# Opening of a wavelet-attention and FFN kernel: chunks 2 and 3 analysed by even and odd tokens

## The reference

```python
for _ in range(NUM_LEVELS):              # 2
    l = dwconv(low, h_filter)[:, ::2]
    h = dwconv(low, g_filter)[:, ::2]
    highs.append(h)
    low = l
low = linear_attention(low, NUM_HEADS)   # keys = elu + 1, kv = sum of keys * values over all tokens
for h, L in zip(reversed(highs), reversed(lens)):
    low = dwconv(up_l, h_synth) + dwconv(up_h, g_synth)
x = layernorm(x + layer_norm(x + low) ...)
x = layernorm(x + (silu(x @ wg.T) * (x @ wu.T)) @ wd.T)
```

## Time and profile before

| | |
|---|---|
| median of 3 runs | 1214.51 us (1214.37 to 1216.5) |
| the profiled execution, its own time | 1215.94 us |
| its span | 1214.1 us |
| PE, DVE, ACT, POOL busy | 98%, 81%, 55%, 25% |

### The profile page before, as it was taken

One profiled execution on the slowest core, in us unless ns is written; L12 is line 12 of the kernel. 1 busy time (PEld: TensorE's weight loads), 2 busy tenths in 40 slices (PEclk: granted clock), 3 DMA queues, 4 the chain that ended last, 5 costly groups with the idle time before them and its releaser, 6 DMA issues.

```text
span 1214.1 us, 19304 instructions
## 1 busy us (share of the span) xinstructions
PE 1188.0 (98%) x6352; PEld 622.1 (51%) x6352; DVE 984.6 (81%) x1981; ACT 672.3 (55%) x1395; POOL 303.7 (25%) x730
## 2 busy tenths in 40 slices
PE   7989999999999999999999999999999999999997
PEld 6868644455445544455444444454445444454443
DVE  7997999998999989996997779867997689845331
ACT  5853754578446853577346644566346644565342
POOL 0013223052223413052122413142213313131101
PEclk9999999999999999999999999999999999999999
DMA  6777421213202220212102210211111310110000
GB/s 233 240 185 161 161 64 56 96 62 132 71 27 96 96 71 18 96 61 97 35 27 96 75 57 19 101 66 53 35 47 75 105 33 12 41 56 1 8 29 35
DMA packets 51869, 91.86 MB, mean 76 GB/s; under 512 B 8896, under 2 KB 28608, under 8 KB 50880
## 3 DMA queue, kind: packets, MB, share of 16 engines
q1 hardware_dynamic: 50048, 86.01, 21.3%
q0 software_dynamic: 1728, 4.72, 2.2%
HBM read 65.99 MB, written 25.19 MB: 75 GB/s over the span
## 4 chain that ended last, share of the span: by engine, by line
PE 82%; DVE 7%; ACT 4%; issue 3%; POOL 2%; DMA 1%; SPq 0%; POOLq 0%; DVEq 0%; ACTq 0%
PE ps_up L641 12%; PE ps_up L642 12%; PE ps_gate L641 12%; PE ps_gate L642 12%; PE ps_down L659 12%; PE ps_down L660 12%; PE ps_x L584 2%; PE ps_y L602 2%; DVE l L1229 1%; DVE h L1229 1%; DMA q_scratch<-keys 1%; PE ps_x L563 1%; POOL rs L1158 1%; PE ps_down L806 1%; DVE hid L1229 1%
## 5 line engine op out<-in xcount | busy, mean ns | idle before, releaser
L659 PE MATMUL ps_down<-w,hid 128*128 128x512 f16 x768 | 291.2, 379 | 1.2 <-DVE hid L1618 1.0
L660 PE MATMUL ps_down<-w,hid 128*128 128x512 f16 x768 | 291.1, 379 | 0.0
L641 PE MATMUL ps_up<-x_hi,w 128*128 128x512 f16 x760 | 288.2, 379 | 1.0 <-DVE h_f L1631 1.0
L641 PE MATMUL ps_gate<-x_hi,w 128*128 128x512 f16 x760 | 288.2, 379 | 0.5 <-ACT h_f L1102 0.5
L642 PE MATMUL ps_gate<-x_lo,w 128*128 128x512 f16 x760 | 288.1, 379 | 0.0
L642 PE MATMUL ps_up<-x_lo,w 128*128 128x512 f16 x760 | 288.1, 379 | 0.0
L1102 ACT ACTIVATE h_f<-ps_gate 128x512 f32<-128x512 f32 x192 | 113.9, 593 | 205.2 <-PE ps_gate L642 204.2
L1631 DVE SCALAR_TENSOR_TENSOR h_f<-ps_up,h_f 128x512 f32<-128x512 f32 x192 | 130.9, 685 | 110.4 <-PE ps_up L642 97.6
L1094 ACT ACTIVATE hid<-h_f 128x512 f16<-128x512 f32 x192 | 119.8, 624 | 42.5 <-DVE h_f L1631 42.4
L1618 DVE TENSOR_TENSOR hid<-h_f,hid 128x512 f16<-128x512 f32 x192 | 130.9, 682 | 1.9 <-ACT hid L1094 1.0
L641 PEld LDWEIGHTS ps_up<-x_hi,w 128*128 128x128 f16 x760 | 74.4, 98 | 91.4 <-DVE h_f L1631 1.9
(11 more groups left out here) (247 smaller groups left out, 1728.5 us busy)
## 6 DMA issues: line engine op xcount, KB each, us to landing
xt<-x_tok SPq DMA_DIRECT2D x64, 256.0 KB, 2.6
out<-x SPq DMA_DIRECT2D x64, 256.0 KB, 2.0
xa<-x_chan SPq DMA_DIRECT2D x28, 515.0 KB, 5.2
xb<-x_chan SPq DMA_DIRECT2D x7, 2060.0 KB, 7.6
w<-weights POOLq DMA_DIRECT2D x12, 384.0 KB, 9.7
att<-den SPq DMA_DIRECT2D x32, 129.5 KB, 2.7
q_in<-q_scratch SPq DMA_DIRECT2D x7, 518.0 KB, 4.8
h_in<-h_scratch SPq DMA_DIRECT2D x7, 518.0 KB, 5.8
```

The costliest lines, as they stand in the source:

```text
L641: pe.matmul(ps_gu[k % 2][g][:, :], w, x1_hi[:, b, c, :], start=(c == 0), stop=False)
L659: pe.matmul(ps_d[t % 2][:, :], h_hi[:, k, t * P:(t + 1) * P], w, start=(k == 0), stop=False)
L660: mm = pe.matmul(ps_d[t % 2][:, :], h_lo[:, k, t * P:(t + 1) * P], w, start=False, stop=(k == NH - 1))
```

## The change

- **x in another layout.** For chunks 2 and 3 of rounds 0 to 4 the host also gives `x_phase`. A chunk is split in two halves h of 64 channels; the even tokens of such a half lie in partitions 0 to 63, the odd ones in 64 to 127. `load_pro` takes its place in SP's list, with the same bytes. Round 0's copy lies in `x1`, so `xb` of chunks 2 and 3, which the closing reads, is loaded with two more DMAs of 515 KB behind rounds 1 and 2.
- **Two taps in one matrix.** `phase_diag(c, h, n)` is 128x64: 64 channels out, and both parities in, so it carries two taps. `conv1` and `conv2` write even outputs (or half 0) to partitions 0 to 63 of a bank and odd ones (or half 1) to 64 to 127, which are two column groups of the array, in turn. A chunk takes 8 matmuls of 257 or 256 columns as before, each on half of the array's columns. Rounds 0, 3 and 4 add one matmul of one column for each half, which writes the edge's zero. The constants come with a DMA (`phase_sb`) between `coef` and `ident`.
- **Chunk 2 of level 2** goes from DVE and ACT to PE: `conv2(a, 2)` behind `pro_kv(a-1)`, into ps_down1, with `pro_out2_copy(a, 2)`. `pro_band_taps(a, 2)` and `pro_band_firsts(a, 2)` are gone. kv moves from ps_down1 to ps_x.
- **Order of ACT.** `pro_l1(a+1, 0)` and `(a+1, 1)` stand at the end of round a, ahead of `pro_keys(a, 0)`. `pro_diags` makes 28 matrices instead of 24, ten in each of rounds 1 and 2, eight in round 3.

The core of the diff:

```diff
+        def phase_diag(c, h, n):
+            at = (c - 2) * 8 * P + (h * 4 + n) * HALF
+            return diag_z[:, at:at + HALF]
...
+        def l1_phase_of(a, c):
+            return l1_of(a)[:, c, :].rearrange("p (h n) -> p h n", h=2)
...
             sp.dma_start(coef[:, :, 0:16], taps).then_inc(ld_taps, 16)
+            sp.dma_start(phase_sb[:, :], phase).then_inc(ld_taps, 16)
             sp.dma_start(ident[:, :], identity).then_inc(ld_taps, 16)
...
+                if a in (1, 2):
+                    sp.dma_start(xb[:, a + 1, :], x_chan[:, 0, a + 1, :]).then_inc(ld_xb0, 16)
...
-                pro_conv(ps_gu[c - 2], xb if a == 0 else xa, c, 0, span_l1(a)).then_inc(pro_conv1, 1)
+                x = x_phase_of(a, c)
+                for h in range(2):
+                    bank = ps_gu[c - 2][h]
+                    spans = [[0, LP], [0, LP]]
...
+                    for k in range(2):
+                        for out_phase, (lo, hi) in enumerate(spans):
+                            r = out_phase + k
+                            mm = pe.matmul(bank[out_phase * HALF:(out_phase + 1) * HALF, lo:hi], phase_diag(c, h, k),
+                                           x[:, h, 2 * lo + r:2 * (hi - 1) + r + 1:2], start=(k == 0), stop=(k == 1))
+                mm.then_inc(pro_conv1, 1)
+            def conv2(a, c):
...
                 for g in range(2):
-                    for k in range(4):
-                        mm = pe.matmul(ps_d[0][:, g * M2:(g + 1) * M2], diag(3, 4 * g + k),
-                                       l1_of(a)[:, 3, k:k + 2 * M2 - 1:2], start=(k == 0), stop=(k == 3))
+                    for k in range(2):
+                        for h in range(2):
+                            mm = pe.matmul(ps_d[3 - c][h * HALF:(h + 1) * HALF, g * M2:(g + 1) * M2],
+                                           phase_diag(c, h, 2 * g + k), x[:, h, k:k + M2], start=(k == 0),
+                                           stop=(k == 1))
...
             for a in range(NPRO):
-                pro_l1(a, 0)
-                pro_l1(a, 1)
-                if a > 0:
+                if a == 0:
+                    pro_l1(a, 0)
+                    pro_l1(a, 1)
+                else:
                     pro_keys(a - 1, 1)
...
-                pro_band_firsts(a, 2)
...
-                    pro_diags(8 * (a - 1), 8)
-                pro_out2_copy(a)
+                    pro_diags(10 * (a - 1), 10)
+                pro_out2_copy(a, 3)
+                pro_out2_copy(a, 2)
+                if a < PER_BATCH:
+                    pro_l1(a + 1, 0)
+                    pro_l1(a + 1, 1)
                 pro_keys(a, 0)
...
-                pro_band_taps(a, 2)
                 if 0 < a < PER_BATCH:
                     pro_kv_add(a - 1)
```

More of the change, by code:

```diff
@@ L42 @@
 HEAD = 32
+HALF = P // 2
+XP = XW // 2
+LP = LW // 2
 LN_EPS = 1e-5
@@ L166, with mixer_ffn @@
 COPIES = HEAD // CHUNK_HEADS
-def mixer_ffn(nc, x_tok, x_chan, taps, gamma, beta, edge, weights, identity, block_mask, head_mask, out):
+def mixer_ffn(nc, x_tok, x_chan, x_phase, phase, taps, gamma, beta, edge, weights, identity, block_mask, head_mask, out):
     q_dram = nc.dram_tensor("q_scratch", [P, BATCHES, NC, SEQ // 4 + 3], F32, kind="Internal").ap()
@@ L460, in _ @@
             sp.dma_start(coef[:, :, 0:16], taps).then_inc(ld_taps, 16)
+            sp.dma_start(phase_sb[:, :], phase).then_inc(ld_taps, 16)
             sp.dma_start(ident[:, :], identity).then_inc(ld_taps, 16)
+            load_pro(0, 3)
+            for c in range(2):
+                sp.dma_start(xb[:, c, :], x_chan[:, 0, c, :]).then_inc(ld_x0[c], 16)
+            load_pro(0, 2)
             for c in (3, 0, 1, 2):
-                sp.dma_start(xb[:, c, :], x_chan[:, 0, c, :]).then_inc(ld_x0[c], 16)
-            for c in (3, 0, 1, 2):
-                load_xa(1, c)
+                load_pro(1, c)
             for dst, src in ((mask[:, :], block_mask), (head_of[:, :], head_mask),
@@ L719, in pro_turn @@
                     pe.wait_ge(turn_out, NC * (a - 1) + c + 1)
+                if c == 0 and a > 0:
+                    pe.wait_ge(kv_added, a)
                 if c == 2:
@@ L764, in h_conv @@
                     pe.wait_ge(turn_out, NC * PER_BATCH)
[L765 removed]
+                    pe.wait_ge(diag_syn_ready, 8)
+                    pe.wait_ge(ld_xb0, 32)
                 else:
@@ L808, in pro_s @@
                 mm.then_inc(pro_s_mm, 1)
-            pe.wait_ge(ld_taps, 32)
+            pe.wait_ge(ld_taps, 48)
+            pe.wait_ge(set_dve, 1)
             for a in range(NPRO):
@@ L819, in _ @@
                     pro_kv(a - 1)
-                conv2(a)
+                conv2(a, 3)
                 if 0 < a < PER_BATCH:
                     pro_kv(a - 1)
+                conv2(a, 2)
             closing = {"attend": pro_attend, "h_conv": h_conv, "low": pro_low_band, "s": pro_s, "gu": gate_up_half,
@@ L1006, in pro_diags @@
             def pro_diags(first_one, count):
-                todo = [(diag(2, 4 + k), 2, G0 + k) for k in range(4)]
+                todo = [(diag(c, 4 + k), c, G0 + k) for c in (2, 3) for k in range(4)]
                 todo += [(syn_diag(c, n), c, n) for c in (2, 3) for n in SYN]
@@ L1041, in pro_low_band @@
                         copy(dst, (ps_d, ps_gu[1])[half][c - 2][:, first_col:first_col + hi - lo]).then_inc(done, 1)
-            act.wait_ge(ld_taps, 32)
-            for k in range(4):
-                scaled(diag(3, 4 + k), ident[:, :], 3, G0 + k).then_inc(diag_g_ready, 1)
+            act.wait_ge(ld_taps, 48)
+            for c in (3, 2):
+                for h in range(2):
+                    for n in (2, 3):
+                        nc.scalar.activation(phase_diag(c, h, n), phase_sb[:, 0:HALF], ACT.Copy,
+                                             scale=phase_coef(c, h, n)).then_inc(diag_g_ready, 1)
             for a in range(NPRO):
-                pro_l1(a, 0)
-                pro_l1(a, 1)
-                if a > 0:
+                if a == 0:
+                    pro_l1(a, 0)
+                    pro_l1(a, 1)
+                else:
                     pro_keys(a - 1, 1)
@@ L1216, in _ @@
             V.memset(scrap[:, 5:6], 0.0).then_inc(lo_done, RING)
-            dve.wait_ge(ld_taps, 32)
+            dve.wait_ge(ld_taps, 48)
             for c in (3, 2):
-                for k in range(4):
-                    V.tensor_scalar(diag(c, k), ident[:, :], coef[:, c, k:k + 1], None, ALU.mult
-                                    ).then_inc(diag_h_ready, 1)
+                for h in range(2):
+                    for n in range(2):
+                        V.tensor_scalar(phase_diag(c, h, n), phase_sb[:, 0:HALF], phase_coef(c, h, n), None, ALU.mult
+                                        ).then_inc(diag_h_ready, 1)
             for dst, a, b in ((S12, S0 + 1, S0 + 2), (S01, S0, S0 + 1), (S23, S0 + 2, S0 + 3),
@@ L1669 @@
     taps = np.ascontiguousarray(taps.transpose(3, 2, 0, 1).reshape(P, NC, 16))
+    phase = taps[:, 2:4, 0:8].reshape(2, HALF, 2, 2, 2, 2).transpose(5, 1, 2, 0, 3, 4).reshape(P, 4 * NC)
+    phase = np.ascontiguousarray(np.concatenate([np.tile(np.eye(HALF, dtype=taps.dtype), (2, 1)), phase], axis=1))
     gamma = np.ascontiguousarray(np.broadcast_to(np.asarray(L0_attn_norm_gamma), (P, C)))
@@ L1686 @@
     arrays, args = {}, []
-    for name, a in (("x_tok", x.reshape(BATCHES * SEQ, C)), ("x_chan", x_chan), ("taps", taps), ("gamma", gamma), ("beta", beta),
+    for name, a in (("x_tok", x.reshape(BATCHES * SEQ, C)), ("x_chan", x_chan), ("x_phase", x_phase),
+                    ("phase", phase), ("taps", taps), ("gamma", gamma), ("beta", beta),
                     ("edge", edge), ("weights", weights), ("identity", identity), ("block_mask", block_mask),
```

112 lines of the change are left out of this document (60 added, 52 removed).

## The result

| | before | changed |
|---|---|---|
| median of the runs | 1215.51 us (1213.44 to 1216.94) | 1209.07 us (1208.44 to 1209.82) |
| span of the profiled execution | 1214.1 us | 1207.8 us |
| from 0 to the attention on PE | 84.96 | 77.66 |
| from there to the loop's first 128x512 matmul | 50.05 | 51.81 |
| from there to the end | 1079.1 | 1078.3 |

The account below looks back on a forecast made before the run. DVE's work and the path keys sum, store, keys, first tap set the rounds. Round 4 8.6 us earlier, 11.0 without chunk 2's tail, less 0.5 for xt and 0.5 for covers: 10.0, so 1204.5; range 1201.5 to 1210.

Parts of the forecast that it names:

- the 0.5 taken off: Closing: 0.5 us deducted from the gain for several covers of under 1 us, leaving 10.0 us.
- The start: Round 0: twelve DVE taps of level 2 instead of eighteen, from 14.55, so round 1 starts at 19.3, before 21.74.
- the 1.82 us a chunk: PE in the opening: sixteen instructions on two array halves run beside one another, 1.82 us a chunk instead of 3.64.
- ACT as the bound of round 1: Rounds 1 to 3: ACT's work of 12.35 us (11.76 in round 3) exceeds DVE's 10.6 and PE's 9.9.
- the wait of the keys for their store: Rounds: first taps no longer queue behind keys waiting for their store, which is covered by 0.1 to 0.5 us.
- xt: Start of the closing: DVE adds beta to `xt`, whose loads land at 70.4 to 72.4; takes 0.5 us back.
- The rival that the halves run one behind the other: PE in the rounds: a chunk takes 3.64 us, PE becomes the bound, 1225 us in all; chance 0.07.
- the covers of rounds 2 and 3: Rounds: ACT's inputs come 0.1 to 0.9 us before needed; 0.5 us in all for store and added loads.
- the clock, for which the forecast had a chance of 0.16: Clock rival, chance 0.16; its full wording isn't given. A granted clock below 1 before 70 us was a sign of being wrong.
- the rival of the landings: Opening: stores land 1 us later, so keys and band firsts wait, 3 to 3.5 us in all, 1208; chance 0.10.
- The rival by which the gain is given back in the closing: Closing: weights, POOL's small operations or a clock falling elsewhere take the gain back, 1212 to 1216; chance 0.05.
- a clock that stays up behind the attention: Closing: a clock gain of 1.7 us, counted in the range's lower end beside 10.5 and 0.5.

Follow-up runs that it names:

- two kernels whose rounds are the same: Changed kernel plus identity matmuls filling PE's closing gap: twelve with POOL's list unchanged, 1208.59 us; eight with POOL's last five weight DMAs issued later, 1205.67 us.

## Why the prediction was right or wrong

The sum by its own steps, forecast against the profile of the changed kernel:

| step | forecast | measured | missing |
|---|---|---|---|
| DVE's round 1 starts | 19.3 | 19.09 | -0.2 |
| round 1 | 12.35 | 12.38 | 0.0 |
| rounds 2 and 3, with 0.5 for waits | 24.6 | 27.02 | 2.4 |
| round 4 starts | 55.9 | 58.49 | 2.6 |
| from there to the attention on PE | 18.6 | 19.17 | 0.6 |
| attention to loop | 50.05, "the same work with the same waits" | 51.81 | 1.8 |
| loop to the end, and the 0.5 taken off | 1079.1, 0.5 | 1078.3 | -1.3 |

The fourth row is the sum of the first three, and 0.4 more, since the forecast counted ACT's start from 19.5 and took 0.55 off at the end. 2.6 + 0.6 + 1.8 - 1.3 = 3.7, and 10.0 - 3.7 = 6.3, the difference of the two spans.

**Right.** The start; the 1.82 us a chunk, which were taken from the four denominators and measured 1.83; ACT as the bound of round 1, whose parts add up to 12.35 and took 12.38; the wait of the keys for their store gone, without which nothing would have come; xt (0.88 of wait where 0.5 were taken). The forecast put 0.08 us on a change between pieces of the array, and 0.06 fits the trace: sixteen instructions from 25.46, which step by 1.82 in all, should end their stream at 27.28, and kv starts at 27.34. The rival that the halves run one behind the other is out: 0.92 us for eight instructions is half of the 1.82 that eight took on the whole array.

**Wrong in size: the covers of rounds 2 and 3.** The prediction added ACT's parts up, found each wait "met with 0.1 to 0.9 us to spare", and took 0.5 for all of them. They took 0.8 in round 2 and 2.1 in round 3. (ACT idle in the rounds and a granted clock below 1 ahead of 70 us were among the signs of being wrong that the prediction named.) From ACT's row at 45.05 to 58.98, round 3 is 11.8 us of work, 0.6 for the store of h2 and 1.5 for chunk 2 of level 2. The 1.5 is the clock, for which the forecast had a chance of 0.16: PE was idle for 2.29 us in one piece, the granted clock was 0.50 for 3.4 us behind it, transposes and level 2 came late, and so did out2 of chunk 2. Filling that gap gave round 3 back (12.27, 12.43 and 12.51 us in the three kernels with that fill). In each of the three profiles of the changed kernel the clock fell once in the rounds, and twice, in rounds 1 and 2, in two kernels whose rounds are the same; in none did it fall in all three. The trace of before had one fall behind a gap of 2.57 us, at 84.96, and one behind 1.94 us, at 112.51. The 0.6, and 0.7 in round 2, are the rival of the landings, at 1.4 of its 3 to 3.5 us: the forecast looked at how full the queues are, and missed that moving the first taps ahead also starts DVE's round sooner behind the store's issue (0.60 instead of 1.58 us in round 3).

**Wrong in kind: the closing.** "From there the closing is the same work with the same waits, and weights too are asked for earlier, since POOL waits for att." They are, by 5.4 us, as the att DMAs follow round 4. But the work on PE, ACT and DVE came 8.5 us earlier there (ACT's last copy of the high band starts at 96.29, before at 104.83), since the clock that had fallen behind 84.96 stayed at 1.00 in this profile. POOL, with its 15.20 us of stop, had not been late and now was, by 2.7 (97.4 to 100.1), and ACT's wait for it grew from 1.01 to 2.94 us, which is close to the 1.8 that the closing grew by. That made PE's gap 3.12 us, where it had been 1.94, and the clock stayed at 0.50 for 6.8. With a fall in the attention, as in the two other profiles, POOL was late by less, and the closing took 50.81 and 51.18. The row was in the trace of before, as POOL's 15.20 us of "issue"; it lay on no path there and wasn't read. The rival by which the gain is given back in the closing, "by the weights, by POOL's small operations or by a clock that falls at another place", named it, with a chance of 0.05 and as a loss of all or most of the gain (1212 to 1216), without a step of its own.

**A term that no run shows.** The lower end of the range counts 1.7 us for a clock that stays up behind the attention; its upper end takes in the clock (0.16) and the landings (0.10). Where the clock did stay up there, at 1.00 from 77 to 104 us in the first profile of the changed kernel, the closing took 51.81 us, with 6.8 us at 0.50 from 104.6, and not less than the 50.05 of before. What the runs show is another 1.7: the closing with one fall to 0.50 behind PE's later gap against the closing with none (48.87 and 48.89 against 47.21 and 47.22).

**Luck.** The last row gave 1.3 us back. 0.5 of it is the deduction for several covers, which the rows above had used up. The other 0.8 lies in the loop, where nothing was forecast; without it the median would be 1209.9, at the very edge of the range.

**Left open.** Why POOL doesn't issue its eighth DMA until the first seven have moved; that it doesn't is seen in nine profiles, but no run changed the size or number of its DMAs. Why PE stopped in round 4 in two kernels with the fill and not in the third. Where the 0.8 us of the loop went: the twelve profiles with the new layout have 1078.3 to 1078.7 us from the loop's start to the end, the two without it 1079.1 and 1079.4, so it belongs to that part of the change and isn't chance.

## What to carry to other kernels

Where an opening of rounds runs through all engines, write down the loop (who waits for whom once around) beside each engine's sum: the halves took 3.5 us a round from PE and 2.4 from DVE and gave nothing until the first taps stood at an earlier place of that loop. When a stage is to come earlier, list every engine that takes part in the next stage and what it does meanwhile, DMA issues and their stops too; one that is tied to something else becomes late. Work taken from PE also opens gaps, and here the granted clock fell to 0.50 for 3.4 us behind some of them: price the work that follows each new gap at the low clock that the trace of before shows, and look there for the shortest gap with a fall behind it (1.94 us here), not for the longest (2.57).
